# First choice of experts and low parts of tokens moved into the mixtures of a four-layer network

## What is computed

```
for layer in 0..3:
    x = x + conv_layer(norm_c(x))                 # four different parts
    t = tokens(x)                                 # 8192 tokens x 64 channels
    n = (t - mean) / sqrt(var + 1e-5)             # over the 64 channels
    logits = n @ router + bias                    # 16 experts (layers 0, 3) or 8 (1, 2)
    gate = softmax over the two largest logits, 0 elsewhere
    layers 0, 3:  y[e] = (silu(n @ w1[e]) * (n @ w2[e])) @ w3[e]
    layers 1, 2:  y[e] = gelu(n @ W1[e] + b1[e]) @ W2[e] + b2[e]
    t = t + sum over e of gate[e] * y[e]
```

## Time and profile before

| | |
|---|---|
| median of 3 runs | 1943.03 us (1941.33 to 1944.0) |
| profiled execution | 1943.33 us, span 1941.5 us |
| TensorE busy | 1699.2 us, 88% |
| VectorE busy | 1133.1 us, 58% |
| ScalarE busy | 981.2 us, 51% |
| GpSimd busy | 872.0 us, 45% |
| mean granted clock of TensorE | 0.933 of full speed |

### The profile page before, as it was taken

One profiled execution on the slowest core, in us unless ns is written; L12 is line 12 of the kernel. 1 busy time (PEld: TensorE's weight loads), 2 busy tenths in 40 slices (PEclk: granted clock), 3 DMA queues, 4 the chain that ended last, 5 costly groups with the idle time before them and its releaser, 6 DMA issues. The chain is left out here.

```text
span 1941.5 us, 31234 instructions
## 1 busy us (share of the span) xinstructions
PE 1699.2 (88%) x11643; PEld 941.2 (48%) x11643; DVE 1133.1 (58%) x1536; ACT 981.2 (51%) x1415; POOL 872.0 (45%) x740
## 2 busy tenths in 40 slices
PE   5679999999579999807899996999999958999998
PEld 2535555554234444303444442777676724555554
DVE  5666777765863432495443325656555556777765
ACT  3435455554136666422566652666666644555554
POOL 0526777775033333280333335212212015778777
PEclk7889999999799999956899998999999978999999
DMA  5003343334003222200222231000000003333333
GB/s 114 1 1 105 107 109 109 105 110 131 21 1 85 76 86 80 65 0 1 67 78 76 74 95 39 1 2 2 1 2 1 2 2 85 111 116 116 114 115 98
DMA packets 71581, 121.37 MB, mean 63 GB/s; under 512 B 16962, under 2 KB 18690, under 8 KB 70786
## 3 DMA queue, kind: packets, MB, share of 16 engines
q1 hardware_dynamic: 71426, 119.32, 21.3%
HBM read 115.60 MB, written 3.67 MB: 61 GB/s over the span
## 5 line engine op out<-in xcount | busy, mean ns | idle before, releaser
L598 POOL TENSOR_TENSOR x<-x,mx_gated 128x512 f32<-128x512 f32 x256 | 331.6, 1295 | 104.3 <-DVE mx_gated L553 103.8
L546 DVE TENSOR_TENSOR mx_hidden<-mx_second,mx_hidden 128x1024 f32<-128x1024 f32 (+1 forms) x256 | 245.0, 957 | 178.4 <-PE mx_second L427 178.4
L695 ACT ACTIVATE mx_hidden<-mx_first,w_bias 128x1024 f32<-128x1024 f32 x256 | 264.6, 1115 | 125.0 <-PE mx_first L427 124.9
L735 POOL TENSOR_TENSOR x<-x,mx_gated 128x512 f32<-128x512 f32 x128 | 164.5, 1285 | 286.2 <-DVE mx_gated L712 286.2
L712 DVE SCALAR_TENSOR_TENSOR mx_gated<-mx_out,w_bias,mx_gates 128x512 f32<-128x512 f32 x128 | 96.0, 750 | 287.0 <-PE mx_out L669 265.5
L530 ACT ACTIVATE mx_hidden<-mx_first 128x1024 f32<-128x1024 f32 x256 | 248.6, 1022 | 18.7 <-PE mx_first L427 4.5
L1615 DVE TENSOR_TENSOR c_near_weights<-c_near_hats 128x768 f32<-128x768 f32 x192 | 177.6, 966 | 133.1 <-PE c_near_turned L1495 133.1
L494 PE MATMUL mx_out<-mx_hidden,w_second 128*64 128x512 f32 x1024 | 248.4, 605 | 2.3 <-issue 2.3
L427 PE MATMUL mx_first<-tokens_high,w_high 64*128 64x512 f32 x1024 | 217.6, 421 | 23.8 <-PEq L59 23.8
L669 PE MATMUL mx_out<-mx_hidden,w_second 128*64 128x512 f32 x1024 | 233.4, 598 | 0.0
L1569 ACT COPY c_near_matrix<-c_near_turned 128x512 f32<-128x512 f32 x288 | 150.3, 594 | 116.7 <-PE c_near_turned L1495 116.7
(11 more groups left out here) (213 smaller groups left out, 2285.6 us busy)
## 6 DMA issues: line engine op xcount, KB each, us to landing
mx_gates<-gate_board SPq DMA_DIRECT2D x768, 128.0 KB, 3.1
w_first<-in_f_first SPq DMA_DIRECT2D x4, 1024.0 KB, 11.9
c_weight<-in_c_weight SPq DMA_DIRECT2D x1, 2304.0 KB
x<-in_x SPq DMA_DIRECT2D x8, 256.0 KB, 4.7
w_second<-in_f_second SPq DMA_DIRECT2D x4, 512.0 KB, 13.3
w_first<-in_f_first SPq DMA_DIRECT2D x4, 512.0 KB, 9.9
out_x<-x SPq DMA_DIRECT2D x16, 128.0 KB, 2.7
gate_board<-xn SPq DMA_DIRECT2D x16, 64.0 KB, 2.9
```

Of the source, the lines that this page charges most:

```text
L546: dve.tensor_tensor(own, second[:, 0:halves, :], own, ALU.mult).then_inc(s.hidden.semaphore, 1)
L598: pool.tensor_tensor(place, place, gated[:, n % GATED, :], ALU.add).then_inc(s.added.semaphore, 1)
L695: act.activation(hidden[:, n % HIDDEN, f], first[:, (n * F + f) % BLOCKS], ACT.Gelu, bias=w.bias1[:, e * F + f:e * F + f + 1]).then_inc(s. ...
L735: pool.tensor_tensor(place, place, gated[:, n % GATED, :], ALU.add).then_inc(s.added.semaphore, 1)
```

## The change

1. `staggered` is gone; every engine's order in the norm is written out. Three reciprocals instead of two come ahead of the first normalization, and the last pair's `wide` goes into two banks of `mean` that are free by then.
2. Products of the router alternate between two banks (`raw_of`).
3. Operations 0 to 11 of the first choice and its tanh move from the norm into the mixture. In SwiGLU: 0 to 5 first in VectorE's queue, 6 to 11 behind `multiply(0)`, 12 to 16 behind `multiply(1)`; `turn` moves behind the layers of steps 1 to 3 (n == 2). In GELU all seventeen stand first, and `turn` moves behind `first_layer(2)`. In SwiGLU the later choices begin one round later.
4. GpSimd makes only 2 of the 8 low parts in the norm. The other six are made in the mixture, once the first gap is there: all at once in GELU, two a round in three rounds in SwiGLU.

```diff
-            raw = ps("raw", [P, CHUNK])
+            raw_bank = ps("raw", [P, CHUNK])
...
-        def staggered(*stages):
-            last = max(behind for behind, _ in stages)
-            for n in range(PAIRS + last):
-                for behind, stage in stages:
-                    if 0 <= n - behind < PAIRS:
-                        stage(n - behind)
+        def raw_of(n):
+            return raw_bank if n % 2 == 0 else mean[:, 2, :]
+        def wide_of(n):
+            return wide if n < PAIRS - 1 else mean[:, 0:2, :]
...
             def scales(n):
-                if n >= 1:
+                if n == PAIRS - 1:
+                    pe.wait_ge(s.kept, pairs + n)
+                    pe.wait_ge(s.centred, pairs + n)
+                elif n >= 1:
-                    last = pe.matmul(wide[:, q // 2, columns(q)], k.spreading[half(q // 2), q % 2, :],
+                    last = pe.matmul(wide_of(n)[:, q // 2, columns(q)], k.spreading[half(q // 2), q % 2, :],
...
-                if n >= 1:
-                    pe.wait_ge(g.raw_kept, raw_pairs + n)
-                    pe.wait_ge(g.logits, raw_pairs + n)
+                if n == 1:
+                    pe.wait_ge(s.squared, chunks + CHUNKS)
+                    pe.wait_ge(s.centred, pairs + PAIRS)
+                if n >= 2:
+                    pe.wait_ge(g.raw_kept, raw_pairs + n - 1)
+                    pe.wait_ge(g.logits, raw_pairs + n - 1)
-                    last = pe.matmul(raw[quarter(q), 0:COLS], w.router[:], xn[:, at:at + COLS], start=True, stop=True)
+                    last = pe.matmul(raw_of(n)[quarter(q), 0:COLS], w.router[:], xn[:, at:at + COLS], start=True, stop=True)
-                    last = pe.transpose(raw[:, COLS + c * P:COLS + (c + 1) * P],
+                    last = pe.transpose(raw_of(n)[:, COLS + c * P:COLS + (c + 1) * P],
+            means(0)
+            means(1)
+            variances(0)
+            means(2)
+            variances(1)
+            variances(2)
+            scales(0)
+            means(3)
-                staggered((0, means), (4, turns), (1, variances), (2, scales), (3, route))
+                variances(3)
+                scales(1)
+                route(0)
+                scales(2)
+                turns(0)
+                route(1)
+                scales(3)
+                turns(1)
+                route(2)
+                route(3)
+                turns(2)
+                turns(3)
-                staggered((0, means), (1, variances), (2, scales))
+                scales(1)
+                variances(3)
+                scales(2)
+                scales(3)
...
-            def table(n):
-                if n == PAIRS - 1:
-                    act.activation(k.spare[:, 1:2], k.eps[eps][:], w.activation)
...
-                act.copy(kept[:, n % 2, :], raw[:, 0:COLS]).then_inc(g.raw_kept, 1)
+                act.copy(kept[:, n % 2, :], raw_of(n)[:, 0:COLS]).then_inc(g.raw_kept, 1)
+            squares(0)
+            squares(1)
+            deviations(0)
+            squares(2)
+            deviations(1)
+            deviations(2)
+            squares(3)
+            deviations(3)
-                staggered((0, squares), (1, deviations), (1, table), (3, highs), (3, keep))
-                top_two.squash(act, 0)
-            else:
-                staggered((0, squares), (1, deviations))
+                act.activation(k.spare[:, 1:2], k.eps[eps][:], w.activation)
+                highs(0)
+                keep(0)
+                highs(1)
+                keep(1)
+                keep(2)
+                highs(2)
+                keep(3)
+                highs(3)
             @block.gpsimd
             def _(pool):
-                for i in range(CHUNKS):
+                for i in range(EARLY):
...
-                    dve.tensor_tensor(own, own, wide[:, a, :], ALU.mult).then_inc(s.normed, 1)
+                    dve.tensor_tensor(own, own, wide_of(n)[:, a, :], ALU.mult).then_inc(s.normed, 1)
-                turned = raw[:, COLS:CHUNK].rearrange("p (t e) -> p t e", e=SWIGLU.experts)[:, :, 0:E]
+                turned = raw_of(n)[:, COLS:CHUNK].rearrange("p (t e) -> p t e", e=SWIGLU.experts)[:, :, 0:E]
...
+            centres(0)
+            centres(1)
+            scales(0)
+            centres(2)
+            scales(1)
+            scales(2)
+            norm(0)
+            centres(3)
+            norm(1)
+            scales(3)
+            if stats:
+                statistics(0)
+                statistics(1)
+            norm(2)
-                staggered((0, centres), (4, logits), (1, scales), (2, norm))
-                for j in range(12):
-                    top_two.op(dve, 0, j)
-            elif stats:
-                staggered((0, centres), (1, scales), (2, norm), (2, statistics))
+                logits(0)
+            if stats:
+                statistics(2)
+            norm(3)
+            if router:
+                logits(1)
+                logits(2)
+                logits(3)
+            if stats:
+                statistics(3)
-            else:
-                staggered((0, centres), (1, scales), (2, norm))
+EARLY = 2
...
+def token_low(k, pool, tokens, i):
+    pool.tensor_tensor(tokens[1][:, chunk(i)], k.xn[:, chunk(i)], tokens[0][:, chunk(i)].bitcast(F32),
+                       ALU.subtract).then_inc(k.gt.low, 1)
+def lows(k, i):
+    return k.mixtures * (CHUNKS - EARLY) + i - EARLY + 1
...
     def keep(self, act, i, turned):
+        if i >= EARLY:
+            act.wait_ge(self.k.gt.low, lows(self.k, i))
     def post(self, sp, i):
...
     def _(pe):
         def first_layer(n):
+            if e == 0 and n // E >= EARLY:
+                pe.wait_ge(k.gt.low, lows(k, n // E))
...
             second_layer(n)
-            if n == 0:
+            if n == 2:
                 gates.turn(pe, 0, out[:, turn_slot(0), :])
...
             if n == 1:
+                top_two.squash(act, 0)
+            if n == 3:
                 gates.keep(act, 0, out[:, turn_slot(0), :])
...
-        for j in range(12, top_two.OPS):
-            top_two.op(dve, 0, j)
         def choose(pair, at):
-            if at < 2:
-                top_two.op(dve, pair, 2 * at)
-                top_two.op(dve, pair, 2 * at + 1)
-            elif at <= 8:
+            if 1 <= at <= 3:
+                top_two.op(dve, pair, 2 * at - 2)
+                top_two.op(dve, pair, 2 * at - 1)
+            elif 4 <= at <= 8:
...
+        for j in range(6):
+            top_two.op(dve, 0, j)
         for n in range(0, STEPS, 2):
             if n >= 2:
                 multiply(n - 1)
+            if n == 2:
+                for j in range(12, top_two.OPS):
+                    top_two.op(dve, 0, j)
...
             multiply(n)
+            if n == 0:
+                for j in range(6, 12):
+                    top_two.op(dve, 0, j)
...
+        pool.wait_ge(k.gt.gap, k.mixtures * top_two.PAIRS + 1)
         for n in range(2, STEPS + 2, 2):
             multiply(n - 1)
+            if n <= CHUNKS - EARLY:
+                token_low(k, pool, tokens, EARLY + n - 2)
+                token_low(k, pool, tokens, EARLY + n - 1)
...
     def _(pe):
         def first_layer(n):
+            if e == 0 and n // E >= EARLY:
+                pe.wait_ge(k.gt.low, lows(k, n // E))
...
             first_layer(n)
+            if n == 2:
+                gates.turn(pe, 0, out[:, turn_slot(0), :])
             first_layer(n + 1)
-            if n == 0:
-                gates.turn(pe, 0, out[:, turn_slot(0), :])
...
+            if n == 0:
+                top_two.squash(act, 0)
...
-        for j in range(12, top_two.OPS):
+        for j in range(top_two.OPS):
...
     @block.gpsimd
     def _(pool):
+        pool.wait_ge(k.gt.gap, k.mixtures * top_two.PAIRS + 1)
+        for i in range(EARLY, CHUNKS):
+            token_low(k, pool, tokens, i)
...
+        self.low = new("gt_low")
```

## The result

The changed kernel takes 1953.07 us (median of 4 runs, 1951.57 to 1954.32) beside 1942.40 for the kernel before on the same chip (4 runs): a ratio of 1.0055, interval 1.0039 to 1.0071. It is slower by 10.7 us. Its profiled execution took 1951.57 us, with a span of 1949.8 and a mean granted clock of 0.940 (before 0.933).

The account below looks back on a forecast made before the run. It took TensorE as the mixtures' bound, standing still at the seams, with GpSimd three quarters full. SwiGLU +7.4, GELU +3.8 and norms without a router -4.8 gave +6.4 us: 1949.5 us, own range 1946 to 1955, 8-in-10 range 1933 to 1957.

Parts of the forecast that it names:

- The seam: From a router norm's first product to its mixture: 23.0 us, 6.1 us earlier in SwiGLU and 4.8 in GELU.
- SwiGLU, +3.7 each: Each SwiGLU norm with its mixture: moved choice and low parts cost 3.7 us net, +7.4 for both.
- first gate: SwiGLU mixture: first gate starts 18.7 us in; its lateness alone loses 1.5 us.
- end of the third layer of step 7: SwiGLU mixture: GpSimd's queue of twelve operations behind the first gate ends this layer at 35.9 us, 3.1 us slower.
- GELU, +1.9 each: Each GELU norm with its mixture: +0.2 us from the late start plus 1.7 for the clock, +3.8 for both.
- first second layer: GELU mixture: begins 13.8 us in, against 8.8 before.
- the low clock: GELU mixture: the clock may fall in the new 5 us wait for `turn` and stay low behind it; priced 1.7 us.
- The lock: Mixture starts: VectorE's last choice operations and GpSimd's operations hold each other, alternating one for one; GELU's five end at 10.7 us.
- The first rival: Mixture starts: VectorE hardly held; SwiGLU 0, GELU -3.8, norms -4.8, so -12.4 us, 1931; chance 0.30.
- Norms without a router, -4.8: Four norms without a router: new order saves 1.7 us in each of three, layer 0's +0.3, together -4.8.
- The order and the two banks in a router's norm: Norm with a router: new order and two banks by themselves make it only 0.4 us shorter.

Follow-up runs that it names:

- E7: E2 with VectorE's multiply of step 3 moved ahead of the gates of steps 0 and 1 in SwiGLU; 1929.11 us, ratio 0.9930.
- E8: E7 with GpSimd's half of the step 3 multiply right behind the low parts, ahead of the first add; 1928.38 us, ratio 0.9927.
- E6: E2 with choice, tanh and `turn` of SwiGLU layers back at their old places, four low parts before GpSimd's first multiply, two behind; 1929.05 us, ratio 0.9932.
- E1: Changed kernel with all eight low parts made in the norm, the choice still in the mixture; 1949.47 us, ratio 1.0028.
- E4: Changed kernel with first choice, tanh and `turn` where they were before, only the six low parts moved; 1945.64 us, ratio 1.0021.
- E2: Changed kernel with GpSimd making the six low parts in a row once the first gates are computed, in SwiGLU ahead of the first add; 1930.35 us, ratio 0.9929.
- E5: Changed kernel with 16 full-height filler products ahead of `turn` in GELU layers, results overwritten; 1952.37 us, ratio 1.0053.
- E3: Kernel before with only the norms' new order and the two banks; choice, tanh and low parts as before; 1942.05 us, ratio 1.0001.

## Why the prediction came out as it did

The forecast of 1949.5 us, slower, had the mechanism right in its steps; the span grew by 8.3 us where +6.4 stood. That the two are so near is in part luck: 4.1 of the 8.3 us lie in the first products of the norms, at a clock that the forecast had left out, and its own terms came to +4.9, with -0.7 outside them.

**The seam.** Forecast 23.0 us in every norm with a router; measured 22.83, 24.43, 24.63 and, in layer 1, 25.63. The order of the work was laid out rightly: at full clock a norm is 3.67 + 19.16 = 22.83 us long in SwiGLU and 22.69 in GELU (layer 1 of E7). What the forecast left out is the clock at the start of a norm. In layers 2 and 3 it is low there before and after. In layer 1 TensorE idles 3.22 us ahead of the norm in both kernels; in the kernel before its first 8 products then take 3.67 us, in the changed one 6.61, at half clock. E7 has this norm at full clock and 22.69 us long, E8, which differs from it by the place of one instruction of GpSimd in SwiGLU layers, at half and 25.65. So these 3 us come and go without a change in the order of the norm's work. What decides it, no run tested; the moment in the execution alone does not (546.24 us half in E6, 546.36 full in E7, 546.68 half in E8).

**SwiGLU, +3.7 each.** Measured +3.1 and +4.6. Its steps: `turn` at 12.05 us forecast, 11.5 measured; first gate 18.7, 18.4; end of the third layer of step 7 35.9, 36.25; GpSimd without a gap from its first add, as said. The choice of that layer as the mark, and of GpSimd's queue as what sets it, was right. But the weights were wrong. I took GpSimd's low parts for the cause and the first gate for a small part (1.5 us). Taking the low parts out of the mixtures (E1) gives back 2.8 and 1.8 us there (its mixtures also start at the low clock) and costs 2.9 in each norm: 0.1 and 1.1 us worse in sum. Taking the choice out (E4) gives back 3.0 and 2.6 us per norm with its mixture, and E2 shows TensorE waiting 3.76 us behind the first gate. So the late gate costs the SwiGLU layers more than GpSimd's queue does.

**GELU, +1.9 each.** Measured +3.5 and +0.9; without the first products of the norms (+2.9 and -0.6) they are +0.6 and +1.5. `turn` at 10.8 forecast, 10.3 measured; first second layer 13.8, 14.5; the low clock fell in the wait and stayed behind it, at a price of 1 to 2 us (E5), where 1.7 stood. The mixtures came out 5.7 and 6.6 us longer against 6.7 forecast (4.8 + 1.9), so this term was right within 1. The Trainium skill ("TensorE: Matmul & The Clock Gate", part 1) says that it is idleness that sends the array to its lower clock; E5 agrees: with the idle time filled, 0.51 became 1.00.

**The lock.** The first rival had VectorE hardly held, 1931. In GELU the five operations took 1.09 to 1.30 us each beside six low parts in a row, and 0.17 to 0.29 with none (E1), so the rows of single operations carried over to a queue of six, one for one. 1931 is nevertheless what E2 reached, by making GpSimd wait. Not every operation is held. VectorE of the changed kernel, layer 0, beside the two low parts from 158.06 to 160.77:

```profile
158.43 0.42 DVE L353 TENSOR_REDUCE gt_place<-gt_rank 128x16 f32<-128x256 f32 x1
158.76 1.22 DVE L617 TENSOR_TENSOR mx_hidden<-mx_second,mx_hidden 128x1024 f32<-128x1024 f32 x1
```

The reduction and the multiply with an input from PSUM take their usual times. The Trainium skill ("SBUF — State Buffer", who interferes with whom) says of reductions that they never contend, and of operations with two inputs from SBUF that they do; the trace agrees with both.

**Norms without a router, -4.8.** Measured -3.1 (+0.62, -1.67, -1.75, -0.28), but this again is the start of the norms: behind the first 8 products the changes are 0.0, -1.4, -1.8 and -1.4, -4.6 in sum, so the term was right. In layer 3 the chain at the end of the norm is shorter by the 2.1 us that the earlier trace rows and their answer show, and the norm began at the low clock, at 1.20 us for its first product.

**The order and the two banks in a router's norm.** Forecast 0.4 us shorter. E3 shows them 0.4 to 0.6 longer there. In the changed kernel this does not show, since the work at the end of the norm has left it.

**The sum.** Forecast +6.4, measured +8.3 between the spans. The forecast's terms are -21.8 for the seams, +33.0 for the mixtures and -4.8 for the norms without a router. Measured behind the first products they are -22.8, +32.3 and -4.6; convolutions and start add -0.7, and the first products +4.1. The medians lie 10.7 apart and not 8.3: the profiled run of the changed kernel is the fastest of its four, 1.5 us below their median, and that of the kernel before (1943.33) is 0.9 above its.

## What to carry to other kernels

Work that is taken out of a gap between two stages must be followed to its first consumer: in the GELU mixtures the gates are needed 9 us in, and hiding their choice pays 2 us a layer alone (E1 against E3) and 5 together with the low parts (E2 against E3), in profiled norm and mixture; in the SwiGLU ones they are needed at once, and it pays nothing in any order tried. Two moves into the same stretch must be costed together and ordered there: six low parts that wait for the five small operations of VectorE, and don't run beside them, made 23 us of difference in the median over four layers, 16 between the profiled spans. And where one wait goes, look for the next in the same queue before expecting the whole gain (E2, E7, E8).

## What the hardware showed

- VectorE's operations of 16 columns with one tensor input and its operations with two tensor inputs from SBUF were held beside GpSimd's: 0.17 and 0.29 us became 1.09 to 1.30. In queues on both sides they took turns, one for one: in layer 1 five operations of VectorE against six low parts, 1.25 us per pair, and GpSimd lost nothing (7.53 us for six, 1.27 each alone). In layer 0, against operations of 256 columns, it lost a little: 2.84 us for two.
- The low clock after an idle stretch lasted 10.2 us in the kernel before (573.3 to 583.5) and 6.8 in the changed one, twice. The same idle time of 3.22 us before the norm of layer 1 was followed by full clock in two profiled runs (before, E7) and by half in the other eight, and cost 2.9 us there: 8 products in 6.61 us and not 3.67.
- The first eight products of all eight norms together took 39.0 us (before) to 44.4 (E1) in the ten profiles, and nothing else in a norm with the same code differed by more than 0.05 us. Whether this makes the scatter between runs of one kernel (1 to 10 us) was not tested.
